# Attention scores in 32x32 TensorE tiles over the columns that a block needs, with masks in the same row groups, and a few steps of the opening, the closing and the first expert pair reordered

## What is computed

```
x = x + 0.5 * ffn(layernorm(x))        # 16 experts, top-1 routing, capacity 320, 128 -> 512 -> 128 with gelu
x = x + attn(layernorm(x))
x = x + 0.5 * ffn(layernorm(x))

# attn: 8 heads on 4 key/value heads of 16, rope on q and k
scores = einsum('bhtd,bhsd->bhts', q, k) * SCALE
scores = scores + head_scales * (qp[..., :, None] * kp[..., None, :])   # qp, kp: first 3 dims along a fixed direction
allowed = (j <= i) & ((j < 4) | (j >= i - 128 + 1))                     # a window of 128 keys, and 4 sinks
attn = softmax(where(allowed, scores, -inf)); out = (attn @ v) @ Wo
```

## Time and profile before

| | us |
|---|---|
| median of 3 runs | 532.63 (531.9 to 535.16) |
| the profiled execution | 535.43 |
| its span | 533.6 |
| routing, 0 to 69.5 | 69.5 |
| first expert stage, to 159.3 | 89.8 |
| gap and opening of attention, to 187.4 | 28.1 |
| attention, to 407.7 | 220.3 |
| closing, to 432.9 | 25.2 |
| second expert stage, to the end | 100.7 |

### The profile page before, as it was taken

The page is one execution under the profiler, slowest core; times in us unless marked ns, Lnnn a source line. Parts: engine busy times, 40 slices in busy tenths (PEclk is TensorE's granted clock), DMA queues, the critical chain, the costliest instruction groups (busy, mean ns, idle before and its releaser), DMA issues.

```text
span 533.6 us, 11602 instructions
## 1 busy us (share of the span) xinstructions
PE 446.6 (84%) x3532; PEld 298.6 (56%) x3537; DVE 283.4 (53%) x1526; ACT 249.3 (47%) x563; POOL 223.7 (42%) x289
## 2 busy tenths in 40 slices
PE   2556079999967789999999999999989679999990
PEld 1445047666643455667566666666655337666660
DVE  3775323333422667676968786878584532333321
ACT  3444123443430456575666666565656405344330
POOL 5576600553463455060544444441214510355464
PEclk9999999999998899999999999999999889999996
DMA  8824124555541360000001010000010124554520
GB/s 276 248 94 168 40 79 139 162 153 156 154 138 57 99 225 2 2 22 2 21 12 33 11 33 13 17 26 28 17 32 18 47 60 125 151 160 140 173 77 25
DMA packets 46499, 45.85 MB, mean 86 GB/s; under 512 B 6859, under 2 KB 35684, under 8 KB 46416
## 3 DMA queue, kind: packets, MB, share of 16 engines
q1 hardware_dynamic: 41840, 37.00, 22.6%
q0 software_dynamic: 4608, 8.22, 4.6%
HBM read 29.49 MB, written 19.17 MB: 91 GB/s over the span
## 4 chain that ended last, share of the span: by engine, by line
PE 44%; DVE 7%; issue 4%; ACT 3%; POOL 2%; another core or an unknown queue 1%; DMA 1%; POOLq 0%; DVEq 0%; ACTq 0%
PE sc L720 9%; PE sc L606 6%; PE b L784 4%; DVE junk L1339 4%; PE b L616 3%; PE sc L712 3%; PE sc L727 3%; PE b L595 2%; PE b L765 2%; PE b L794 2%; ACT probs L1045 2%; PE sc L537 1%; PE b L685 1%; PE b L560 1%
## 5 line engine op out<-in xcount | busy, mean ns | idle before, releaser
L1339 DVE CUSTOM_DVE_ANT_0 junk<-sc,cht 128x256 bf16<-128x256 f32 (+1 forms) x256 | 84.7, 387 | 40.9 <-PE sc L720 39.4
L980 ACT ACTIVATE hT<-sc 128x320 f32<-128x320 f32 x128 | 55.9, 437 | 51.1 <-PE sc L606 34.9
L1546 POOL DMA_INDIRECT slots<-pay,slot_i x64 | 63.6, 994 | 38.3 <-issue 16.2
L606 PE MATMUL sc<-enT,w1s 128*128 128x320 f32 x256 | 74.8, 436 | 0.7 <-issue 0.4
L616 PE MATMUL b<-hT,w2s 128*128 128x320 f32 x256 | 73.8, 432 | 0.0
L1045 ACT ACTIVATE probs<-sc 128x1024 f32<-128x1024 f32 x48 | 49.3, 1026 | 44.2 <-PE sc L727 44.0
L720 PE MATMUL sc<-qkT 32*128 32x256 f32 (+1 forms) x512 | 65.8, 374 | 0.0
L727 PE MATMUL sc<-qnT,qkT 32*128 32x256 f32 x448 | 65.6, 404 | 0.0
L1566 POOL DMA_INDIRECT x<-yrow,ytok x40 | 38.9, 972 | 58.8 <-DVE yrow L1308 48.2
L1566 POOL DMA_INDIRECT out<-yrow,ytok x40 | 38.9, 972 | 58.7 <-DVE yrow L1308 49.0
L606 PEld LDWEIGHTS sc<-enT,w1s 128*128 128x128 f32 x256 | 47.5, 190 | 21.4 <-issue 3.4
(11 more groups left out here) (147 smaller groups left out, 778.1 us busy)
## 6 DMA issues: line engine op xcount, KB each, us to landing
w1s<-in_L_ffn_w SPq DMA_DIRECT2D x32, 256.0 KB
w2s<-in_L_ffn_w SPq DMA_DIRECT2D x32, 256.0 KB
slots<-fresh SPq DMA_DIRECT2D x16, 330.0 KB, 5.5
rows<-slots SPq DMA_DIRECT2D x16, 330.0 KB
xall<-in_L_attn_x SPq DMA_DIRECT2D x8, 256.0 KB
xall<-x SPq DMA_DIRECT2D x8, 256.0 KB, 2.9
out<-xall SPq DMA_DIRECT2D x8, 256.0 KB
slots<-pay,slot_i POOLq DMA_INDIRECT x64
```

What stands on the lines that cost most here:

```text
L606: mm(hid[f], w1s[a][:, P * f:P * (f + 1)], enT[:, :, HALF * a:HALF * (a + 1)], start=True, stop=True).then_inc(e_hid, 1)
L980: nc.scalar.activation(hT[a][:, f, :], hid[f], ACT.Gelu_apprx_tanh).then_inc(e_gelu, 1)
L1339: ins = v.tensor_tensor_reduce(junk[:, head, lo:], sc[h][:, jj, 2 * P * g + lo:2 * P * (g + 1)], table[:, lo:], scale=1.0, scalar=MASKED, ...
L1546: gp.indirect_dma_start(out=slots_d[phase], out_offset=bass.IndirectOffsetOnAxis(ap=slot_i[s][:, t:t + 1], axis=0), in_=pay[s][:, t, :], i ...
```

## The change

Scores: each product `score` and `turned_score` of 128 rows becomes four products of 32 rows (`c` in `range(KV)`), each over its own range of columns. The turned scores' order of the two key blocks is swapped for the lower two row tiles. `masks` takes its table from the row group of the head (`at = RG * (2 * h + jj)`), from tables laid out anew (160 columns for each row tile, side by side), and the rolled tables go. `qkT` is laid out as [q of group 0, q of group 1, k][block], so that the keys of two neighbouring blocks are contiguous. Block 1 keeps the whole width where sinks are needed.

Before attention the 40 filling products go into all four score banks, ten each. Opening: `warm(6)` becomes `warm(11)`; GpSimd waits for VectorE's first bend before `rope(0, 1)`. Closing: GpSimd scatters one tile, then does the second reciprocal root, then scatters three. First pair: its rows load in two transfers (three chunks, two chunks) with a semaphore each; TensorE transposes three chunks into b4 and two into b5; VectorE copies the first, ScalarE the second. The scaling of the q weights and `fresh_ranks` move ahead of `experts(0)` on VectorE.

```diff
@@ -34,6 +34,7 @@
...
 PC = 2 * CAP // P
+EARLY = 3
 FC = FF // P
...
@@ -86,12 +87,12 @@
...
     addh("window", np.concatenate([prev, own], 1))
-    addh("turned_window", np.concatenate([prev.T, own.T], 1))
     prev_sinks = np.where(p[None, :] < SINKS, 0.0, prev)
     addh("window1", np.concatenate([prev_sinks, own], 1))
-    addh("turned_window1", np.concatenate([prev_sinks.T, own.T], 1))
-    addh("rolled_window", np.roll(np.concatenate([prev.T, own.T], 1), HALF, 0))
-    addh("rolled_window1", np.roll(np.concatenate([prev_sinks.T, own.T], 1), HALF, 0))
+    for name, before in (("turned_window", prev), ("turned_window1", prev_sinks)):
+        turned = np.concatenate([before.T, own.T], 1)
+        part = np.concatenate([turned[RG * c:RG * (c + 1), RG * c:P + RG * (c + 1)] for c in range(KV)], 1)
+        addh(name, np.tile(part, (KV, 1)))
     addh("upto", p[:, None] <= p[None, :])
...
@@ -251,7 +252,7 @@
...
         dscaled = sb("dscaled", [P, TB, H])
-        qkT = sb("qkT", [P, TB, 3 * P])
+        qkT = sb("qkT", [P, G + 1, TB, P])
         qnT = [sb(f"qnT{i}", [P, G, P]) for i in range(2)]
...
@@ -476,7 +480,8 @@
...
                 sp.wait_ge(fresh_out[phase], 16 * PAIRS)
-                sp.dma_start(rows[:, 0], slots_p[phase][0]).then_inc(rows_in, 16)
+                sp.dma_start(rows[:, 0, 0:EARLY], slots_p[phase][0][:, 0:EARLY]).then_inc(early_in, 16)
+                sp.dma_start(rows[:, 0, EARLY:], slots_p[phase][0][:, EARLY:]).then_inc(rows_in, 16)
...
@@ -590,9 +595,12 @@
...
                     wait(pe, e_rows, (max(g - 2, g0) if isinstance(p, int) else g - 2) * PC)
+                    n = EARLY if isinstance(p, int) and p == 0 else 4
                     for c in range(PC):
                         pe.wait_ge(e_xn, g * PC + (c + 1))
-                        last = turn(b4[:, P * c:P * (c + 1)] if c < 4 else b5[:, 0:P], en[:, c, :], ident)
+                        last = turn(b4[:, P * c:P * (c + 1)] if c < n else b5[:, P * (c - n):P * (c - n + 1)], en[:, c, :], ident)
+                        if n == EARLY and c == n - 1:
+                            last.then_inc(e_early, 1)
                     last.then_inc(e_turned, 1)
...
@@ -600,6 +608,8 @@
...
                         pe.wait_ge(e_xT, g + 1)
+                        if isinstance(p, int) and p == 0:
+                            pe.wait_ge(e_early_xT, phase + 1)
                     for f in range(FC):
...
@@ -669,7 +679,9 @@
...
-            warm(40)
+            for h in range(2):
+                for jj in range(2):
+                    warm(10, sc[h][:, jj, :])
...
@@ -705,26 +717,36 @@
...
                     bank = sc[h][:, jj, :].rearrange("p (g k) -> p g k", g=G)
-                    table = tab16[("rolled_window" if jj else "turned_window") + ("1" if t == 1 else "")]
+                    table = tab16["turned_window1" if t == 1 else "turned_window"]
+                    at = RG * (2 * h + jj)
                     for c in range(KV):
                         lo, hi = RG * c if t else P, P + RG * (c + 1)
-                        at = (RG * c + HALF * jj) % P
+                        part = (P + RG) * c - RG * c
                         mm(bank[RG * c:RG * (c + 1), :, lo:hi], identb[at:at + RG, at:at + RG],
-                           table[at:at + RG, lo:hi].unsqueeze(1).to_broadcast([RG, G, hi - lo]),
+                           table[at:at + RG, part + lo:part + hi].unsqueeze(1).to_broadcast([RG, G, hi - lo]),
                            start=True, stop=False, skip_group_check=True)
...
             def score(t, j, g):
-                lo = 0 if t else P
                 rows_j = slice(RG * j, RG * (j + 1))
                 bank = sc[j // 2][:, j % 2, :].rearrange("p (g k) -> p g k", g=G)
-                return mm(bank[:, g, lo:2 * P], qkT[rows_j, t, P * g:P * (g + 1)],
-                          qkT[rows_j, t - 1:t + 1, G * P:] if t else qkT[rows_j, t, G * P:],
-                          start=(g == 0), stop=(g == G - 1), skip_group_check=True)
-
-            def turned_score(t, j, kb):
+                keys = qkT[rows_j, G, max(t - 1, 0):t + 1].rearrange("p t k -> p (t k)")
+                skipped = 0 if t else P
+                for c in range(KV):
+                    lo, hi = (RG * c if t > 1 else 0) if t else P, P + RG * (c + 1)
+                    last = mm(bank[RG * c:RG * (c + 1), g, lo:hi], qkT[rows_j, g, t, RG * c:RG * (c + 1)], keys[:, lo - skipped:hi - skipped],
+                              start=(g == 0), stop=(g == G - 1), skip_group_check=True)
+                return last
+
+            def turned_score(t, j, i):
+
                 rows_j = slice(RG * j, RG * (j + 1))
-                bank = sc[j // 2][:, j % 2, :].rearrange("p (g b q) -> p g b q", b=2, g=G)
-                return mm(bank[:, :, kb], qkT[rows_j, t - 1 + kb, G * P:], qnT[t % 2][rows_j], start=False, stop=(kb == 1), skip_group_check=True)
+                bank = sc[j // 2][:, j % 2, :].rearrange("p (g b q) -> p g b q", g=G, b=2)
+                for c in range(KV):
+                    kb = i if c < KV // 2 or not t else 1 - i
+                    lo, hi = (RG * c, P) if kb else (0, P if t == 1 and c == 0 else RG * (c + 1))
+                    last = mm(bank[RG * c:RG * (c + 1), :, kb, lo:hi], qkT[rows_j, G, t - 1 + kb, RG * c:RG * (c + 1)], qnT[t % 2][rows_j][:, :, lo:hi],
+                              start=False, stop=(i == 1), skip_group_check=True)
+                return last
...
@@ -754,7 +776,7 @@
...
                 for g in range(G):
-                    last = mm(b7s[:, KV * SINKS * g:KV * SINKS * (g + 1)], qkT[:, t, P * g:P * (g + 1)], ksink[:, :],
+                    last = mm(b7s[:, KV * SINKS * g:KV * SINKS * (g + 1)], qkT[:, g, t, :], ksink[:, :],
                               start=(g == 0), stop=(g == G - 1), skip_group_check=True)
...
@@ -864,7 +886,7 @@
...
                 a_project(0, -2, 1)
-                warm(6)
+                warm(11)
                 turn_qk(0, 0, 0, -1, 4)
...
@@ -971,6 +993,10 @@
...
+                act.wait_ge(e_turned, g0 + 1)
+                wait(act, e_hid, g0 * (2 * FC))
+                nc.scalar.copy(enT[:, EARLY:, :].rearrange("p c q -> p (c q)"), b5[:, 0:P * (PC - EARLY)]).then_inc(e_xT, 1)
+
                 def gelus(p, a):
...
@@ -1031,7 +1057,7 @@
...
                 act.wait_ge(qk_turned, d + 1)
-                nc.scalar.copy(qkT[:, td, :], b4[:, 0:3 * P]).then_inc(qk_copied, 1)
+                nc.scalar.copy(qkT[:, :, td, :], b4[:, 0:3 * P].rearrange("p (i k) -> p i k", i=G + 1)).then_inc(qk_copied, 1)
...
@@ -1282,15 +1308,26 @@
...
                     g = p + g0
-                    dve.wait_ge(rows_in, (g + 1) * 16)
+                    first_pair = isinstance(p, int) and p == 0
+                    if first_pair:
+                        dve.wait_ge(early_in, (phase + 1) * 16)
+                    else:
+                        dve.wait_ge(rows_in, (g + 1) * 16)
...
                     for c in range(PC):
+                        if first_pair and c == EARLY:
+                            dve.wait_ge(rows_in, (g + 1) * 16)
                         r = rows[:, bass.ds(p, 1), c, :].rearrange("p a w -> p (a w)")
...
                     g = p + g0
+                    if isinstance(p, int) and p == 0:
+                        dve.wait_ge(e_early, phase + 1)
+                        wait(dve, e_hid, g * (2 * FC))
+                        v.tensor_copy(enT[:, 0:EARLY, :].rearrange("p c q -> p (c q)"), b4[:, 0:P * EARLY]).then_inc(e_early_xT, 1)
+                        return
                     dve.wait_ge(e_turned, g + 1)
...
@@ -1318,13 +1355,13 @@
...
-            experts(0)
             dve.wait_ge(weights_in, 16 * N_WEIGHTS)
...
             fresh_ranks()
+            experts(0)
...
@@ -1358,7 +1395,7 @@
...
                 wait(dve, ps_ready, b * ST)
-                k0 = qkT[:, 0, G * P:G * P + SINKS].unsqueeze(1).to_broadcast([P, KV, SINKS])
+                k0 = qkT[:, G, 0, 0:SINKS].unsqueeze(1).to_broadcast([P, KV, SINKS])
                 v.tensor_tensor(ksinkb[:, :, 0:SINKS], k0, tab["sink_rows1"].rearrange("p (j s) -> p j s", s=SINKS), ALU.mult)
...
@@ -1593,6 +1630,7 @@
...
                 rstds(1, aveps, arstd, a_var, a_rstd)
+                pool.wait_ge(a_bent, 1)
                 rope(0, 1)
...
@@ -1634,9 +1672,9 @@
...
                 rstds_of_half(0)
-                scatter(LAST - 1, (B - 2) % PAYS, 1, (0, 1, 2))
+                scatter(LAST - 1, (B - 2) % PAYS, 1, (0,))
                 rstds_of_half(1)
-                scatter(LAST - 1, (B - 2) % PAYS, 1, (3,))
+                scatter(LAST - 1, (B - 2) % PAYS, 1, (1, 2, 3))
                 for h in range(2):
...
```

More of the change, by code:

```diff
@@ L284, in macaron @@
         rows_in = sem("rows_in")
+        early_in = sem("early_in")
         w1_in = [sem("w1a_in"), sem("w1b_in")]
@@ L314, in macaron @@
         e_xT = sem("e_xT")
+        e_early = sem("e_early")
+        e_early_xT = sem("e_early_xT")
```

## The result

The changed kernel takes 547.89 us (median of 4 runs, 541.37 to 552.13); beside it the kernel before takes 533.28. The ratio, taken from the fast runs alone (without the slowest of the four), is 1.023, 95% interval 1.013 to 1.033: slower by some 2%, where 5% faster was forecast. The profiled execution took 548.38 us, its span is 546.4.

The account below looks back on a forecast made before the run. TensorE was taken to bound the kernel through attention's half-steps. Scores 21.2 us (after 1.2 off for unseen waits), opening 0.9, first pairs 1.4 and closing 3.0 sum to 26.5, from 532.63 to 506 us; range 499 to 524.

Parts of the forecast that it names:

- Sixteen tiles at once: Scores in attention: 16 small 32x32 tiles run at once, so a tile streams its two passes in 0.54 us against 0.86.
- The starts of the tiles: Scores in a half-step: starting the tiles one after another costs 0.08 us, of 0.85 in all, a saving of 0.48.
- Fresh scores ready at +0.87: Half-step in attention: fresh scores ready about 0.87 us after the masks start, where the first maximum starts at +1.44 now.
- VectorE's bound of 9.24 for half-steps 3 to 5: Middle batch: VectorE's maxima keep these three half-steps from being shorter than 9.24 us, saving 0.89 instead of TensorE's 0.99.
- Half-step 7 to 2.38: Middle batch: ScalarE is last here and had waited idle for only 0.48 us, so 0.41 goes, from 2.79 to 2.38.
- Hidden waits: Attention stage: 1.2 us taken off the saving for unseen semaphore waits, met by TensorE's queue with four times the products.
- Opening: Before attention: more fillings, GpSimd's second rotation waits for VectorE's first bend; turn 0.6 us sooner, 0.9 with the small scores.
- First pairs: First pair of each expert stage: rows load in two transfers, first product sooner; 1.4 us together, 0.6 if the second lands later.
- Closing: End of attention: GpSimd scatters one tile instead of three before the last reciprocal root; 3.0 us taken, between 2.36 and 3.6.
- A: Rival: tile starts are paced at 23 ns, slower, 551 us; decides from 17 ns a start on; chance 0.08.
- B: Rival: only eight tiles run at once, a half-step is 1.25 us and 0.08 is saved; 522 us; chance 0.13.
- C: Rival: VectorE takes the gain back, last in all half-steps but two, a batch saves about 1.6; 514 us; chance 0.14.

Follow-up runs that it names:

- the small parts alone: Kernel before with all of the change but the scores (masks, score products, tables and qkT as before): 530.78 us, ratio 0.988.
- free scores: Changed kernel with each score product over 8 columns (scores left out) and the 24 scatters inside attention left out: 521.99 us.

## Why the prediction was wrong

**What bounds the kernel** was read rightly: TensorE, through the half-steps. But "nowhere else" hid a delay of some 0.5 us in ScalarE's exponentials that was in the profile of before and cost nothing there.

**Sixteen tiles at once** is borne out for twelve: 12 products, each in its own tile, start in 0.13 us. **The starts of the tiles** are the step that failed. They were put at 0.08 us, with masks that start 4 ns apart as the measure (3.3 in the single records). Those are the head of a queue that had filled while TensorE did the work before; behind the first 64 instructions a product of four comes every 17 ns, after a hole of up to 0.15. A half-step of 144 instructions is thus at least 0.80 long, and since its last tiles, which carry the widest products, start at +0.80 and then stream two passes each, 1.34. The saving of 0.48 was 0. Over the stage, undisturbed, 2.1 us (224.23 to 222.11) came of the forecast 21.2. It would be 3.4 without a loss that the small parts bring: in every kernel that has them the clock is at its lower level for 3.4 us or more between 189 and 205 us, and from the third masks of batch 0 to the fourth 4.0 us or more pass, where the kernel before, with scatters or without, takes 3.16 at full clock; with the small parts alone the stage lasts 225.53. What in the opening brings that fall about was not separated.

**The terms under it.** Masks and fresh scores beside each other: right (0.03). Fresh scores ready at +0.87 instead of +1.44: in an undisturbed batch the first maximum comes at +1.21 in the sixth half-step, whose fresh block is a full one, and at +1.40 in the first. The +0.97 of the seventh is no gain of that size: its fresh half is block 0, and the kernel before had +1.05 there. The prediction took the seventh and eighth half-steps for regular ones. VectorE's bound of 9.24 for half-steps 3 to 5, masks to masks: right in kind, 9.43 in batch 3 when the scores are nearly free (2.80, 2.69, 3.94), 9.61 as changed, 10.13 before. Half-step 7 to 2.38: 2.79 as changed, 2.30 with free scores. The middle batch of 25.85 that these terms give lies only 0.6 us above what products of 8 columns take (25.25): with this number of instructions nearly all streaming of columns would have had to hide.

**Hidden waits, 1.2 us.** This allowance was mis-sized as much as the starts: it is 20.8, and with the 19.1 us that the scores failed to save it makes up the 39.9 us between the forecast and the measured stage. Its cause is not TensorE's semaphore waits but GpSimd's scatters, which the prediction counted in the closing alone, and the granted clock, which stood in its last sentence as what "would undo the sum in another way": 10.2 us at the lower level in batch 4.

**Opening**, 0.9 forecast. VectorE's dscaled takes 0.17 instead of 0.85 with GpSimd waiting, and the stretch from the first `up` to the first scores 1.9 less. With the small parts alone it took 1.5 more, with the clock at its lower level for 13.7 us of the opening instead of 6.8; so its own gain isn't told apart. **First pairs**, 1.4 forecast: 0.92 + 0.99 = 1.9 in this execution. In the other runs with this part the two stretches last 6.25 to 7.13 and 6.10 to 7.13 us, against 7.2 to 7.3 and 7.1 to 7.2 in the two without it, so the gain varies from nothing to 1.1 in each. **Closing**, 3.0 forecast, 3.6 the bound given: 3.85 with the small parts alone, 0.5 in the changed kernel, 1.2 with 64-row tiles and two scatters held back. In the changed kernel four scatters stand in a row while the last masks wait, ScalarE is idle for 3.98 us ahead of its exponential, TensorE for 2.21 behind it, and the clock is then low for 6.8 us. ScalarE and GpSimd of the changed kernel:

```profile
421.16 1.02 ACT L1071 ACTIVATE probs<-sc 128x1024 f32<-128x1024 f32 x1 [3.98 <-remote]
```
```profile
415.49 1.04 POOL L1583 DMA_INDIRECT slots<-pay,slot_i  x1 [0.20 <-issue]
...
419.39 0.97 POOL L1583 DMA_INDIRECT slots<-pay,slot_i  x1 [0.30 <-issue]
```

**The rivals.** A (starts are paced, 551) came nearest in time, by luck, and its threshold of 17 ns a start was a sound one to name; but per pass it is 8.4 ns, half the threshold, and without the scatters' part the kernel takes 527.5. It was priced from the wrong row: products that follow one another in one bank. The 25 ns between starts that the Trainium skill states ("Wait — 56ns, not 53.3ns?" in "TensorE: Matmul & The Clock Gate") holds neither for masks (3.3) nor for products of two passes (17) here. B (eight tiles at once, 522) is out: twelve products start in 0.13 us. C (VectorE takes it back) is the bound that would have come next. No rival had the scatters.

What stays open is the path by which a scatter holds up TensorE. The runs show that it does; in two stalled half-steps (298.38 and 363.36) no packet of the instruction queue is on its way (one ends at 297.85, the next starts at 305.53; 362.40 and 368.41), so TensorE didn't wait for such a packet there. Beyond that the path was not found. Nor was it tried how the third and fourth scatter of a batch could be placed at no cost, which could win the 1.5 us of the stage that lie between the 64-row kernels with two scatters held back and with none.

## What to carry to other kernels

Before a product is split into tiles, count the instructions of a burst, not the columns: here up to 64 came at once and each further f32 product cost 17 ns, so that with the scatters left out halving the tile to 64 rows won 8.5 us of the stage and quartering it 2.1 (with two scatters held back 64 rows won 7.0). A saving on one engine takes the slack from every delay that was hidden behind it: look in the trace of before for consumers that start late although their producer had long finished, since such a delay is next. Keep GpSimd's scatters away from dense TensorE sequences, and look at what stands behind them in GpSimd's queue before moving them.

## What the runs showed of the hardware

- A scatter by GpSimd (some 1.0 us) stops a dense sequence of small products for mostly 0.45 to 0.7 us at a time, and delays TensorE's semaphore updates by some 0.5 us (128-row products) to 1.9 (64-row tiles).
- TensorE starts 64 queued instructions in 0.19 us (0.32 at the lower clock), pauses up to 0.15, then starts one every 4.2 ns, at either level of the clock.
- The pause of a scatter comes without a packet of the instruction queue on its way (half-steps at 298.38 and 363.36).
- Alternating groups of 32x32 and 32x128 products cost 0.7 us a half-step more (2.06 against 1.34).
- An operation of VectorE on 4 elements a row took 2.58 us beside GpSimd's rotation, 0.16 to 0.3 in the changed kernel.
